# Two graph attention layers: two of four heads of a group transposed in 32x32 blocks by VectorE, with a scratch in the device's memory

## What is computed

```
h = relu(layernorm(x));  Q, K, V = h Wq' + bq, h Wk' + bk, h Wv' + bv      (8 heads of 32)
scores = where(adj == 0, -inf, Q K' / sqrt(32));  attn = softmax(scores)
x = x + (attn V) Wo' + bo
h = relu(layernorm(x));  e = leaky_relu((h * a_0) h')
alpha = softmax(where(adj == 1, e, -9e15));  x = x + alpha h
```

## Time and profile before

| | |
|---|---|
| time, median of 3 runs | 3796.97 us (3796.73 to 3805.19) |
| profiled execution: span from its first to its last instruction | 3783.3 us |
| the median's distance to that span | 13.7 us |
| TensorE busy, of the span | 3454.1 us, 91% |
| VectorE busy | 2850.7 us, 75% |
| ScalarE busy | 2464.4 us, 65% |
| GpSimd busy | 1125.2 us, 30% |
| mean granted TensorE clock | 0.974 of full |
| moved by the transfer engines | 294.99 MB, 27.0% of their time |

### The profile page before, as it was taken

One profiled execution on the slowest core, in us unless ns is written; L12 is line 12 of the kernel. 1 busy time (PEld: TensorE's weight loads), 2 busy tenths in 40 slices (PEclk: granted clock), 3 DMA queues, 4 the chain that ended last, 5 costly groups with the idle time before them and its releaser, 6 DMA issues.

```text
span 3783.3 us, 97534 instructions
## 1 busy us (share of the span) xinstructions
PE 3454.1 (91%) x34096; PEld 2916.1 (77%) x34096; DVE 2850.7 (75%) x5622; ACT 2464.4 (65%) x4548; POOL 1125.2 (30%) x568
## 2 busy tenths in 40 slices
PE   5889999899998999999899998999989999998975
PEld 4678778787787878778787787877878787787864
DVE  4777778787787878878777787878778787887752
ACT  4775767657676676766757676666766757676541
POOL 2232423323232232423323232232422324233212
PEclk8999999999999999999999999999999999999988
DMA  4141412314132141412414132141321414123101
GB/s 120 51 113 54 128 36 81 93 58 122 40 103 72 59 121 55 112 53 67 107 54 128 40 100 75 54 125 49 110 57 56 122 54 128 40 86 89 37 27 44
DMA packets 166740, 294.99 MB, mean 78 GB/s; under 512 B 25536, under 2 KB 75968, under 8 KB 166080
## 3 DMA queue, kind: packets, MB, share of 16 engines
q1 hardware_dynamic: 166080, 286.63, 27.0%
HBM read 169.09 MB, written 16.78 MB: 49 GB/s over the span
## 4 chain that ended last, share of the span: by engine, by line
PE 61%; issue 11%; ACT 10%; SPq 7%; DVE 7%; DMA 2%; POOL 0%; DVEq 0%; ACTq 0%; POOLq 0%
PE pT L1082 15%; PE pG L1017 13%; PE pG L1095 11%; PE pG L1152 8%; PE ps L1070 7%; SPq L250 6%; ACT sm L490 4%; PE pT L1143 3%; PE pG L1051 3%; DMA adj_half<-in_adj_dram 2%; ACT pt L501 2%; DVE sm L754 1%; DVE pt L766 1%; PE pG L1108 1%; ACT sm L546 1%
## 5 line engine op out<-in xcount | busy, mean ns | idle before, releaser
L754 DVE CUSTOM_DVE_ANT_0 sm<-ps,bias 128x1024 f32<-128x1024 f32 x1024 | 1244.1, 1215 | 20.6 <-issue 17.0
L1082 PE MATMUL pT<-ident,sm 128*128 128x128 f32 x8192 | 1099.7, 276 | 127.0 <-ACT pt L501 108.9
L1082 PEld LDWEIGHTS pT<-ident,sm 128*128 128x128 f32 x8192 | 946.5, 141 | 345.0 <-ACT sm L490 140.4
L490 ACT ACTIVATE sm<-sm,mn 128x1024 f32<-128x1024 f32 x1024 | 1180.5, 1153 | 48.5 <-DVE mn L754 48.0
L501 ACT COPY pt<-pT 128x512 f32<-128x512 f32 x1024 | 596.3, 582 | 592.6 <-PE pT L1082 592.4
L766 DVE COPY pt<-pT 128x512 f32<-128x512 f32 x1024 | 703.0, 687 | 287.1 <-PE pT L1082 281.4
L417 POOL TENSOR_SCALAR gbias<-adj_half 128x512 bf16<-128x512 int32 x256 | 505.2, 1973 | 1324.3 <-DVE mn L865 1030.1
L1070 PE MATMUL ps<-ks,qs 96*128 96x512 f32 x2048 | 760.9, 453 | 76.7 <-DVE mn L754 64.1
L400 POOL TENSOR_SCALAR bias<-adj_half 128x512 bf16<-128x512 int32 x256 | 492.5, 1924 | 785.5 <-DMA adj_half<-in_adj_dram 712.0
L1095 PE MATMUL pG<-pt,v 128*32 128x128 f32 x16384 | 530.7, 283 | 27.5 <-DVE x L889 18.5
L1095 PEld LDWEIGHTS pG<-pt,v 128*32 128x32 f32 x16384 | 455.1, 114 | 87.9 <-issue 39.3
(11 more groups left out here) (104 smaller groups left out, 3328.1 us busy)
## 6 DMA issues: line engine op xcount, KB each, us to landing
adj_half<-in_adj_dram SPq DMA_DIRECT2D x512, 256.0 KB, 2.9
ks<-parts SPq DMA_DIRECT2D x384, 128.0 KB, 2.4
qs<-parts SPq DMA_DIRECT2D x384, 128.0 KB, 2.6
x<-in_x_dram SPq DMA_DIRECT2D x16, 1024.0 KB, 5.6
out_dram<-x SPq DMA_DIRECT2D x128, 128.0 KB, 2.6
x<-in_x_dram SPq DMA_DIRECT2D x32, 256.0 KB, 3.5
rb<-in_x_dram SPq DMA_DIRECT2D x16, 256.0 KB, 3.2
sq<-in_x_dram SPq DMA_DIRECT2D x16, 256.0 KB, 3.3
```

What stands on the lines that cost most here:

```text
L490: nc.scalar.activation(sm[:, ring(t), :], sm[:, ring(t), :], ACT.Exp, scale=-1.0, bias=mn[:, t:t + 1], accum_out=den[:, t:t + 1]).then_inc ...
L754: nc.vector.tensor_tensor_reduce(out=sm[:, ring(t), :], in0=ps[t % 2][:, :], in1=bias[:, node, :], scale=1.0, scalar=3e38, op0=ALU.add, op ...
L1082: last = nc.tensor.transpose(pT[c][:, j * P:(j + 1) * P], sm[:, ring(t), m * P:(m + 1) * P], ident[:, :])
```

## The change

**What it does.** `SWAPPED` are the groups 2 to 9 of each stage. In them the first two tiles (`TURNED`) are not transposed by TensorE. VectorE transposes each 32x32 block of the tile into `turned` (L872). Blocks are then in the wrong partitions, so SP writes `turned` in four transfers of 256 KB to the scratch `bounce` in the device's memory (L327), waits until they have landed, and reads 1 MB back into the first two places of `pt` (L332), from where `values` takes it. The third and fourth tile of such a group are transposed as before, and ScalarE copies both their halves. The values of these groups stand one slot later, ahead of the edge product in slot 4g+5; sums, results and norms move with them by a slot. `turned` has the memory of the weights `wqk` of q and k, which are parked once in the unused partitions 96 to 127 of `ks` and brought back once a stage (`restore`) before the first `qk`.

```diff
+SWAPPED = tuple(range(2, 10))
+BATCH = 4 * 16
+TURNED = tuple(HG * g + h for g in SWAPPED for h in range(2))
+PLAIN = tuple(t for t in range(TILES) if t not in TURNED)
+LATE = tuple(t for t in range(NT) if EDGE // HG + 1 + t in SWAPPED)
...
     for g in range(1, GROUPS - 1):
-        behind[HG * g + HG].append(("av", g))
+        if g in SWAPPED:
+            ahead[HG * g + HG + 1].append(("av", g))
+        else:
+            behind[HG * g + HG].append(("av", g))
...
         for t in range(NT):
-            behind[EDGE + 4 + 4 * t].append(("sum", t))
+            behind[EDGE + (5 if t in LATE else 4) + 4 * t].append(("sum", t))
...
+            def park(back):
+
+                for a in range(4):
+                    spare, part = ks[ROWS:P, 2 * a:2 * a + 2, :].rearrange("p h n -> p (h n)"), wqk[HD * a:HD * (a + 1), :]
+                    if back:
+                        sp.dma_start(part.bitcast(F), spare.bitcast(F)).then_inc(w_back, 16)
+                    else:
+                        sp.dma_start(spare.bitcast(F), part.bitcast(F)).then_inc(parked, 16)
+
+            def swap_blocks(b, g):
+
+                sp.wait_ge(turn_made, len(TURNED) * b + turned_before(HG * g + 2))
+                settle(sp)
+                sp.wait_ge(av, GROUPS * b + g)
+                settle(sp)
+                half, n = g % 2, SWAPPED.index(g)
+                for a in range(4):
+                    sp.dma_start(bounce[half, :, :, :, a, :].rearrange("c j h w -> j h c w"),
+                                 turned[HD * a:HD * (a + 1), :, :, :, :].rearrange("p h c m j -> p h c (m j)")
+                                 ).then_inc(bounced, 16)
+                sp.wait_ge(bounced, BATCH * (len(SWAPPED) * b + n + 1))
+                settle(sp)
+                sp.dma_start(pt[:, 0:2, :, :].rearrange("p h m n -> p (h m n)"),
+                             bounce[half].rearrange("c j h a w -> (c j) (h a w)")).then_inc(swapped, 16)
...
-                for t in range(4):
-                    edge_adj(o, t, base)
+                edge_adj(o, 0, base)
+                edge_adj(o, 1, base)
+                swap_blocks(b, 2)
+                swap_blocks(b, 3)
+                edge_adj(o, 2, base)
+                swap_blocks(b, 4)
+                edge_adj(o, 3, base)
+                swap_blocks(b, 5)
                 store(o, 0)
                 edge_adj(o, 4, base)
+                swap_blocks(b, 6)
                 store(o, 1)
...
+                if t // HG in SWAPPED:
+                    act.wait_ge(tr[1], len(PLAIN) * b + plain_before(t) + 1)
+                    nc.scalar.copy(pt[:, place(t), NT // 2:, :], pT[1][:, :].rearrange("p (m n) -> p m n", n=P)
+                                   ).then_inc(pt_made[1], 1)
...
-                    copy(b, s, not earlier)
+                    if s not in TURNED:
+                        copy(b, s, not earlier)
...
+            def turn(b, t, first):
+
+                dve.wait_ge(exped, TILES * b + t + 1)
+                if t == TURNED[0] and first:
+                    dve.wait_ge(parked, BATCH)
+                if t % HG == 0 and (t > TURNED[0] or not first):
+                    dve.wait_ge(bounced, BATCH * (len(SWAPPED) * b + SWAPPED.index(t // HG)))
+                settle(dve)
+                nc.vector.transpose(turned[:, t % HG, :, :, :].rearrange("p c m j -> p m c j"),
+                                    sm[:, ring(t), :].rearrange("p (m c j) -> p m c j", m=NT, c=4)
+                                    ).then_inc(turn_made, 1)
...
-                    copy(b, s, not earlier)
+                    if s in TURNED:
+                        turn(b, s, not earlier)
+                    elif s // HG not in SWAPPED:
+                        copy(b, s, not earlier)
...
+                if g in SWAPPED:
+                    pe.wait_ge(swapped, 16 * (len(SWAPPED) * b + SWAPPED.index(g) + 1))
...
+                        if HG * g + h in TURNED:
+                            moving = swap[:, h, :, m, :]
+                        else:
+                            moving = pt[:, place(HG * g + h), m, :]
...
-                    transposes(b, s, not earlier)
+                    if s not in TURNED:
+                        transposes(b, s, not earlier)
```

More of the change, by code:

```diff
@@ L190, in two_graph_layers @@
         settled = sem("settled")
+        bounced = sem("bounced")
+        bounce = nc.dram_tensor("bounce", [2, 4, HD, 2, 4, P * 2], F, kind="Internal").ap()
+        turn_made, parked, w_back = sem("turn_made"), sem("parked"), sem("w_back")
+        swapped = sem("swapped")
         GC = 3 * 3 + 2
@@ L1244, in stage @@
[L1244 to L1252 removed]
+                        product(kind, n, len(PLAIN) * b + plain_before(s))
@@ new lines, in stage @@
+                    for t in range(NT):
+                        if earlier and s == EDGE + (5 if t in LATE else 4) + 4 * t:
+                            pe.wait_ge(lpt[0], NT * o + t + 1)
+                            pe.wait_ge(lpt[1], NT * o + t + 1)
+                    if s not in TURNED:
+                        transposes(b, s, not earlier)
+                    for t in range(NT - 1):
+                        if earlier and s == EDGE + (7 if t in LATE else 6) + 4 * t:
+                            edge_values(o, t, pG[bank("sum", t)], (2, 3))
@@ new lines, in stage @@
+                    for kind, n in behind[s]:
+                        product(kind, n, len(PLAIN) * b + plain_before(s + 1))
+                    if earlier and EDGE + 3 <= s < EDGE + 3 + 4 * NT and s % HG == 0:
+                        pe.wait_ge(pt_made[0], len(PLAIN) * b + plain_before(s + 1))
+                        pe.wait_ge(pt_made[1], len(PLAIN) * b + plain_before(s + 1))
+                        edge_transposes(o, (s - EDGE - 3) // 4)
+                    for t in range(NT - 1):
+                        if earlier and s == EDGE + (6 if t in LATE else 5) + 4 * t:
+                            edge_values(o, t, pG[bank("sum", t)], (1,))
```

156 lines of the change are left out of this document (95 added, 61 removed).

## The result

The changed kernel takes **4409.4 us** (median of 4 runs, 4406.7 to 4414.1), the kernel before in the same session 3796.9 (median of 4). The ratio is 1.162, with a 95% interval of 1.158 to 1.165: slower, by 613 us. The forecast was 4478, with a range from 4200 to 4820 and 95% on slower. The profiled execution has a span of 4404.9 us against 3783.3, 621.6 more.

The account below looks back on a forecast made before the run. TensorE alone was taken to set the pace in slots 13 to 40. Fifteen stages' 632 us plus stage 0's 49 on the 3783.3 us span give 4464; plus 13.7 to the runs' median, 4478 us, range 4200 to 4820.

Parts of the forecast that it names:

- The ring: Serial chain from `values` of one changed group to the next, through TensorE, VectorE, SP and both transfers: 19.95 us against 14.49 before.
- Starts of `values`: Sign on TensorE: in slots 13, 17, ... 41 `values` of successive changed groups would start 19 to 21 us apart.
- the pauses: Sign on TensorE: idle time of 4 to 6 us before `values`, ended by a transfer into `pt`, 15 x 8 times.
- `values` and edge product: TensorE's work in the chain: 3.26 us at full clock, 5.4 with the lowered clock; then 0.23 hand-over to VectorE.
- X: Round trip of a group's blocks through device memory, W + R: 11.9 us, between 10.2 and 14.5.
- W: Way out: four 256 KB transfers to `bounce` until all have landed; 6.3 us, the middle between 5.1 and 7.45.
- R: Way back: one 1 MB transfer from `bounce` into `pt`; 5.6 us, between 5.1 and 7.0.
- The clock: TensorE drops to 1.2 GHz after each idle wait, some 4.4 us a ring; granted clock over the span about 0.85.
- The sum: 42.2 us more in each of fifteen stages with edges, 49 in stage 0: 681 us on the profiled span.
- the removed 223 us: TensorE transposes dropped in 16 tiles a stage, over 16 stages; gained only if TensorE stays the bound, so not subtracted.
- First values: First changed group of a stage with edges: its `values` would start 16.4 us after slot 9 opens.
- The rival that it fits: Transfers fit the four slots, TensorE stays the bound: 5%; decided at X = 8.7 us, all gained below 6.8, 3574 us.

## Why the prediction was right, and where it was off

- **The ring** was the decisive step, and held: two different cuts of it, each with all transfers kept, took 439 and 517 us of the 613 away. Predicted 19.95 us, measured 19.77. Starts of `values` are 18.4 to 20.6 us apart, as means by group (said: 19 to 21), the pauses 4.2 us on the mean (said: 4 to 6; V4, V8 and V9 have 3.5, 3.3 and 1.9), 128 of them.
- **Its terms**, with their hand-overs (the 0.5 us split in three): `values` and edge product 5.4 + 0.23, measured 5.53. Mask 0.70, measured 0.62. Transpose 1.22 + 0.17, measured 1.44 (the transpose itself 1.24). X 11.9 + 0.33, measured 12.18.
- **X was right by luck, through two errors.** W was given 6.3 us, as a middle, and took 7.04; R was given 5.6 and took 5.14. And W's make-up was wrong: it was built as 2.25 fixed plus data, and half the bytes need 3.92, which leaves 0.8. SP's time for issuing the four was put at nothing without a reason; it is 3.48 us, half of W. By the nearest source, the stacks, W would have been 7.45. That came nearer, but the row was misread: its 7.82 us are SP's time for issuing twelve transfers, and the last of them landed 2.5 us after its issue. The low end of 5.1 took the rate of a load into 128 partitions for one out of 32. The Trainium skill ("DMA: Bandwidth & Descriptors", Anatomy of one DMA) gives its fit for transfers that GpSimd issues, and the prediction left that out. All of these are issued by SP, so that 7.0 and 5.1 us are not the 4.4 estimated by it says nothing against the page.
- **The clock.** That `values` runs at a low clock behind each pause held (3.64 us where 1.95 is its length, 0.53 granted). The price was put at 2.14 us a ring. Against the 3.49 us that the earlier trace rows give at full clock the PE part of 5.53 is 2.0 more. With idle products it fell by 1.4 to 1.7, and the ring by at most 1.2. The clock over the span was 0.901, not 0.85, and TensorE's share 79%, not 75%: both were guessed too low, since the window with 0.53 is 7 us of 20 in seven groups, and not in the rest of a stage.
- **The sum.** Between the prediction's own points (slot 9 opens; before, the edge product of slot 41 starts; after, the last changed `values` ends) a stage with edges took 116.3 us before and 157.0 after, 40.7 more, where 42.2 was said; stage 0 took 54 more, where 49 was said. The forecast is 69 us too high: some 21 from the stages, less 5 from stage 0, 9 from what lies outside the span (13.7 taken, 4.5 measured; the profiled run itself took 1.8 us more than its span, and the rest is its distance from the median), and 42 from one step: "the removed 223 us are not subtracted, since they lie in TensorE's pauses", and nothing was given for the time behind group 9. There each of 14 stages came out 2.8 us shorter by these points, 3.8 counted from V9. 1.1 us of it is a removed transpose that lies in no pause: tile 8 is the first turned one, and its eight stood between V0 and V1 (9.7 us before, 8.6 after, 9.7 again with group 2 left alone). 1.5 us lie between V14 and V15, with a cause that stays open.
- **First values** were put at 16.4 us after slot 9 opens and came at 16.1. V1 to V2, 18.4 us, holds that trip; it is the one wait that no cut of the ring removed (18.4 to 18.6 in each kernel with whole trips and no idle products).
- **The rival that it fits** put the floor at 3574 us. It is 3694 without any trip in the change's own order, as TensorE then has other waits, for VectorE's copies and masks among them. That the threshold lies at X = 8.7 us was never tested by X alone. With W + R = 8.5 us (one tile's blocks) the time was that of before, 0.998, but not by the prediction's sum: V1 to V9 took 118.3 us a stage against 115.3, and the rest of a stage gave 3.5 back.
- **What was not seen**: that the four slots nearly hold a 12 us trip once nothing closes a ring. The prediction looked at the order to find the ring, and took the order as given.

## What to carry to other kernels

When an operation becomes a round trip by transfer, write down the whole chain from its consumer to its consumer in the next round, through every engine's list; if it closes, the period is its sum, however few of the engines are full. Then break it by order before shortening it: here moved rows on three engines were worth 637 us with the same bytes, and sending each half as soon as it is made another 81. A queue that is issued in one order closes rings of its own, which show only once the first is open.

## What the runs showed of the hardware

- Four transfers out of 32 partitions each, of 256 KB, let SP go on 7.04 us after the first issue, of 128 KB 3.92: nearly in proportion, 168 GB/s for the difference. 1 MB back into 128 partitions lands after 5.0 us, 512 KB after 4.0.
- SP spends 3.48 us on issuing four transfers of 256 KB and 1.79 on four of 128 KB, so issuing is half of W.
- In the changed kernel, which moves 132 GB/s on the mean in place of 78, transfers that the change doesn't touch land later: adjacency after 3.9 us in place of 2.9, results after 4.8 in place of 2.6. Whether the load or their new place behind the reads does it, no run tells apart.
- VectorE's transpose of 32x32 blocks over 128x1024 elements of four bytes takes 1.24 us, as an ordinary pass over the tile does (1.22).
- A group of idle products holds the clock up (0.970 with 40 and 0.959 with 24, against 0.901 over the span), and costs what it runs over: 40 of them took 4.96 us where the pauses had been 4.2 us, and gave back 54 us where 24 gave 125.
